# A two-layer graph network: second experts and first attention's end in another order, first mixture normalised by ScalarE and GpSimd

## The reference

```python
edge_index = jnp.stack([src, dst])                        # 8192 edges
xn = _layernorm(x)
x = x + _L0_gnn_ref(xn, edge_index, ...) + _L0_mix_ref(xn[None], ...)[0]
x = x + _L0_ffn_ref(_layernorm(x)[None], ...)[0]          # 16 experts, top 2
xn = _layernorm(x)
x = x + _L1_gnn_ref(xn, edge_index, ...) + _L1_mix_ref(xn[None], ...)[0]
x = x + _L1_ffn_ref(_layernorm(x)[None], ...)[0]          # 8 experts, top 2
# _L0_gnn_ref, 3 diffusion steps over the row-normalised adjacency
out = diffusion_weights[0] * h
for i in range(STEPS):
    cur = adj @ cur
    out = out + diffusion_weights[i + 1] * cur
return jax.nn.relu(out)
# _L0_mix_ref, the end: (out - mean) * rsqrt(var + EPS) * gamma
# _L1_gnn_ref: two graph attentions, each followed by
x_new = jax.nn.elu(_layer_norm(x_new, g, beta)); x = x + x_new
# _L1_ffn_ref, per token: gates * (gelu(x @ W1 + b1) @ W2 + b2) over its two experts
```

## Time and profile before

| | us |
|---|---|
| median of 3 timed runs | 223.85 |
| lowest and highest of them | 223.84, 232.37 |
| the profiled execution, its own time | 222.05 |
| span from its first to its last instruction | 220.3 |
| busy TensorE, VectorE, ScalarE, GpSimd in the span | 210.9, 141.2, 63.2, 22.1 |

### The profile page before, as it was taken

One profiled execution on the slowest core, in us unless ns is written; L12 is line 12 of the kernel. 1 busy time (PEld: TensorE's weight loads), 2 busy tenths in 40 slices (PEclk: granted clock), 3 DMA queues, 4 the chain that ended last, 5 costly groups with the idle time before them and its releaser, 6 DMA issues.

```text
span 220.3 us, 2936 instructions
## 1 busy us (share of the span) xinstructions
PE 210.9 (96%) x1031; PEld 142.9 (65%) x1031; DVE 141.2 (64%) x416; ACT 63.2 (29%) x148; POOL 22.1 (10%) x36
## 2 busy tenths in 40 slices
PE   7899999999999999999999999999959999999994
PEld 5685547666589988744646786478724564798641
DVE  3899999968998441432629259796934779653302
ACT  2804584322221012100101169730633321103100
POOL 4860010000111000000150000000300001200000
PEclk9999999999999999999999999999999999999969
DMA  5999799935050500000199000000000000000002
GB/s 164 355 394 358 238 404 416 412 118 176 1 190 4 190 0 3 0 0 0 44 297 405 18 0 1 3 0 0 0 0 3 0 0 0 1 3 0 0 0 95
DMA packets 8957, 23.65 MB, mean 107 GB/s; under 512 B 2408, under 2 KB 2408, under 8 KB 8944
## 3 DMA queue, kind: packets, MB, share of 16 engines
q1 hardware_dynamic: 8656, 23.42, 29.0%
q10 hardware_dynamic: 288, 0.07, 0.1%
HBM read 22.95 MB, written 0.52 MB: 107 GB/s over the span
## 4 chain that ended last, share of the span: by engine, by line
PE 84%; DVE 11%; issue 1%; DMA 1%; ACT 1%; POOL 0%; DVEq 0%
PE bank L1180 17%; PE bank L1154 12%; PE bank L1284 10%; PE bank L1272 10%; PE bank L1229 5%; PE bank L1315 4%; PE bank L1191 3%; PE bank L1235 3%; DVE ring L784 3%; PE bank L1329 2%; PE bank L1236 2%; PE bank L1168 2%; DVE ring L787 2%; PE bank L1220 2%; DMA xa<-in_x 1%
## 5 line engine op out<-in xcount | busy, mean ns | idle before, releaser
L1180 PE MATMUL bank<-raw,xT 128*128 128x512 f32 x88 | 39.3, 595 | 0.0
L1180 PEld LDWEIGHTS bank<-raw,xT 128*128 128x128 f32 x88 | 16.2, 190 | 18.3 <-issue 18.2
L301 POOL TENSOR_TENSOR rstd<-veps,minus_half 128x1 f32<-128x1 f32 x14 | 9.2, 660 | 153.2 <-DVE veps L561 111.1
L1315 PE MATMUL bank<-iota_bf 128*128 128x256 bf16 x155 | 21.5, 286 | 1.6 <-DVE iota_bf L760 1.6
L1284 PE MATMUL bank<-raw,ring 128*128 128x512 f32 x48 | 22.7, 633 | 0.0
L1272 PE MATMUL bank<-xT,raw 128*128 128x256 f32 x96 | 22.1, 384 | 0.0
L784 DVE TENSOR_SCALAR ring<-iota_bf,edges,radix 128x128 bf16<-128x128 bf16 x64 | 20.8, 376 | 0.0
L1315 PEld LDWEIGHTS bank<-iota_bf 128*128 128x128 bf16 x155 | 16.1, 107 | 5.2 <-DVE iota_bf L760 1.6
L1272 PEld LDWEIGHTS bank<-xT,raw 128*128 128x128 f32 x96 | 17.8, 190 | 2.3
L1284 PEld LDWEIGHTS bank<-raw,ring 128*128 128x128 f32 x48 | 9.6, 202 | 12.0 <-issue 11.6
L1191 PE MATMUL bank<-xT,raw 128*128 128x256 f32 x64 | 14.6, 382 | 0.2 <-issue 0.2
(11 more groups left out here) (256 smaller groups left out, 331.6 us busy)
## 6 DMA issues: line engine op xcount, KB each, us to landing
raw<-in_up SPq DMA_DIRECT2D x6, 512.0 KB, 10.6
raw<-in_down SPq DMA_DIRECT2D x6, 512.0 KB, 13.8
raw<-in_k SPq DMA_DIRECT2D x4, 512.0 KB, 5.5
raw<-in_q SPq DMA_DIRECT2D x4, 512.0 KB, 6.3
raw<-in_v SPq DMA_DIRECT2D x4, 512.0 KB, 6.9
raw<-in_out SPq DMA_DIRECT2D x4, 512.0 KB, 6.9
raw<-in_gat SPq DMA_DIRECT2D x4, 512.0 KB, 9.5
raw<-in_gnn SPq DMA_DIRECT2D x2, 512.0 KB, 10.0
```

The source lines that it names most:

```text
L1180: ins = mm(bank[banks[t]][:, :], xT_at(c, t), w.at(c), start=c == 0, stop=c == C - 1)
L1315: mm(half(b, 0), iota_bf[:, 0:P], iota_bf[:, :], start=True, stop=True)
```

## The change

In the first layer VectorE only takes the mixture's statistics and writes minus the mean. ScalarE centres the product and scales it by the root; GpSimd multiplies by `gamma0` and adds `xa`. ScalarE also makes the first term of `diffused`. TensorE's idle turns at the seam go from 29 to 11, and its attention-weight products change places with the first transposes. In the first attention's end VectorE's work is written tile by tile; `centred`, `normal`, `positive` and `negative` being one instruction each; the context product stands between the transposes of the two tiles, which go to other banks; ScalarE's exponentials move ahead. In the second experts the position products and the gates' transposes stand earlier among the `up1` products, 15 of 18 idle turns go, and half of `down1` precedes the bias rows. New semaphores and the tile `minus_mean`, and one-instruction helpers that only get a new argument, are left out below.

```diff
--- before.py
+++ after.py
@@ gpsimd
-            roots(1)
+            for t in range(T):
+                pool.wait_ge(var_ready, T + t + 1)
+                nc.gpsimd.tensor_tensor(rstd[:, t:t + 1], veps[:, t:t + 1], minus_half[:, t:t + 1], ALU.pow)\
+                    .then_inc(rstd_ready, 1)
+                pool.wait_ge(mix_scaled, t + 1)
+                then(nc.gpsimd.tensor_tensor(mixed[:, t, :], mixed[:, t, :], row["gamma0"], ALU.mult))
+                nc.gpsimd.tensor_tensor(mixed[:, t, :], mixed[:, t, :], xa[:, t, :], ALU.add).then_inc(mix_ready, 1)
             roots(2)
             roots(3)
@@ scalar, first layer
+            act.wait_ge(small_in, SMALLS)
+            for t in range(T):
+                nc.scalar.activation(diffused[:, t, :], hr[:, t, :], ACT.Copy, scale=diffusion[:, 0:1])\
+                    .then_inc(diffused_ready, 1)
             act.wait_ge(degree_ready, 1)
+            def mixture(t):
+                act.wait_ge(o_full, t + 1)
+                act.wait_ge(mean_ready, t + 1)
+                nc.scalar.activation(mixed[:, t, :], bank[t][:, :], ACT.Identity, bias=minus_mean[:, t:t + 1])\
+                    .then_inc(mix_centred, 1)
+                act.wait_ge(rstd_ready, T + t + 1)
+                act.wait_ge(mix_centred, t + 1)
+                nc.scalar.activation(mixed[:, t, :], mixed[:, t, :], ACT.Copy, scale=rstd[:, t:t + 1])\
+                    .then_inc(mix_scaled, 1)
+
             diffuse(0, (2, 7))
+            mixture(0)
             diffuse(1, (3, 4))
+            mixture(1)
@@ scalar, second layer
             mix_v(1, (5, 4), (0,))
+            elu(0, (0,))
             mix_v(1, (5, 4), (1,))
             for t in range(T):
                 act.wait_ge(ek_full, 2 + t + 1)
                 copy(ek[:, t, :], bank[2 + t][:, :]).then_inc(ek_ready, 1)
+            elu(0, (1,))
+            xT_part(3, 0)
             act.wait_ge(kinv_ready, 1)
             for m in range(C):
                 act.wait_ge(qT_full, 2 + m // 2 + 1)
                 nc.scalar.activation(qT[:, m, :], half(4 + m // 2, m % 2), ACT.Copy,
                                      scale=kinv[:, m:m + 1]).then_inc(qT_ready, 1)
-            elu(0, (0,))
 
             act.wait_ge(ctx_full, 2)
             for r in range(2):
                 p0, p1 = r * HD, (r + 1) * HD
                 copy(ctxbd[p0:p1, :, p0:p1], bank[3][p0:p1, :].rearrange("p (m n) -> p m n", m=C)[:, :, p0:p1])\
                     .then_inc(ctx_ready, 1)
-            elu(0, (1,))
-
-            xT_part(3, 4)
+
@@ vector, first layer
-            for t in range(T):
-                go(V.tensor_scalar(diffused[:, t, :], hr[:, t, :], diffusion[:, 0:1], None, ALU.mult))
...
                 variance(1, t, bank[t][:, :])
-                go(V.scalar_tensor_tensor(mixed[:, t, :], bank[t][:, :], mv[:, t, 0:1], row["gamma0"],
-                                          ALU.subtract, ALU.mult))
-                settle()
-                dve.wait_ge(rstd_ready, T + t + 1)
-                V.scalar_tensor_tensor(mixed[:, t, :], mixed[:, t, :], rstd[:, t:t + 1], xa[:, t, :],
-                                       ALU.mult, ALU.add).then_inc(mix_ready, 1)
+                V.tensor_scalar(minus_mean[:, t:t + 1], mv[:, t, 0:1], -1.0, None, ALU.mult).then_inc(mean_ready, 1)
 
             mixture(0)
+            dve.wait_ge(diffused_ready, T)
             diffuse(0)
             mixture(1)
             dve.wait_ge(step_read, 2)
             diffuse(1)
             dve.wait_ge(step_read, 4)
-            dve.wait_ge(mix_ready, 2)
 
             def residual(t):
                 dve.wait_ge(step_read, 4 + t + 1)
+                dve.wait_ge(mix_ready, t + 1)
@@ vector, second layer
+            def divided(u, t):
...
+                src = bank[AGG[t][u]][:, 0:4 * (HD + 1)].rearrange("p (h n) -> p h n", h=4)
+                dve.wait_ge(agg_full, 2 * u + t + 1)
+                go(V.reciprocal(mx[:, t, heads], src[:, :, HD]))
+                settle()
+                go(V.tensor_tensor(g_a[:, t, cols].rearrange("p (h n) -> p h n", h=4), src[:, :, 0:HD],
+                                   bc(mx[:, t, heads], [P, 4, HD]), ALU.mult))
+                settle()
+                go(V.tensor_tensor(g_a[:, t, cols], g_a[:, t, cols], row["b1"][:, cols], ALU.add))
...
             q_norm(1)
-            divided(0)
-            divided(1)
-            gat_norm(0, 4)
+            divided(0, 0)
+            divided(0, 1)
+            divided(1, 0)
+            settle()
+            variance(4, 0, g_a[:, 0, :])
+            divided(1, 1)
+            centred(0, 0)
+            normal(0, 0)
+            variance(4, 1, g_a[:, 1, :])
+            centred(0, 1)
             dve.wait_ge(xn_less_one, 1)
-            elu(0, x1g, lambda t: xn[:, t, :], xn, lambda ins: ins.then_inc(xn_ready, 1))
-            xT_part(3, 3)
+            positive(0, x1g, 0)
+            normal(0, 1)
+            negative(0, x1g, 0).then_inc(xn_ready, 1)
+            positive(0, x1g, 1)
+            negative(0, x1g, 1).then_inc(xn_ready, 1)
+            xT_part(3, 1)
@@ tensor, seam of the first layer
             attention_weights(0, 6, 0)
-            idle_turns(5, 7)
+            idle_turns(5, 3)
             attention_weights(0, 6, 1)
-            idle_turns(5, 7)
-            attention_weights(0, 6, 2)
             idle_turns(5, 3)
             pe.wait_ge(step_read, 4)
             xT_made(1, xn, (4, 5), (0,))
+            attention_weights(0, 6, 2)
+            idle_turns(5, 3)
             attention_weights(0, 6, 3).then_inc(wa_full, 1)
-            idle_turns(5, 12)
+            idle_turns(5, 2)
             xT_made(1, xn, (4, 5), (1,))
@@ tensor, end of the first attention
             qT_made((4, 5))
+            xT_made(3, x1g, (0, 1), (0,))
             pe.wait_ge(ek_ready, 4)
             context(3)
-            pe.wait_ge(qT_ready, 2 + C)
-            xT_made(3, x1g, (4, 3), (0,))
-            pe.wait_ge(ctx_ready, 4)
-            xT_made(3, x1g, (4, 3), (1,))
+            xT_made(3, x1g, (0, 1), (1,))
             node_rows(1, 7, 3)
             gat2 = Weight("gat2")
             weights_in(gat2)
+            pe.wait_ge(qT_ready, 2 + C)
+            pe.wait_ge(ctx_ready, 4)
@@ tensor, second experts
             logits(5, 1, 4)
-            up("up1", 0, 2)
-            up("up1", 2, 3, (0, 1))
+            up("up1", 0, 1)
+            up("up1", 1, 2, (0, 1))
             positions(1, 6)
-            up("up1", 2, 3, (2, 3))
+            up("up1", 1, 2, (2, 3))
+            up("up1", 2, 3, (0, 1, 2))
+            gate_rows(1, 7)
+            up("up1", 2, 3, (3,))
             up("up1", 3, C, (0, 1))
+            gate_spread(1, (2, 5))
             up("up1", 3, C, (2, 3))
-            idle_turns(2, 12)
-            gate_rows(1, 7)
-            idle_turns(2, 6)
-            gate_spread(1, (2, 5))
+            idle_turns(7, 3)
+            for t in range(T):
+                down("down1", t, bank[3 + t][:, :], C, 1, False, range(0, 2))
             pe.wait_ge(b_down_ready, 1)
             for t in range(T):
                 dst = bank[3 + t][:, :]
                 cols = slice(t * P, (t + 1) * P)
                 g_hi, g_lo = gateT_hi[0:EXPERTS[1], cols], gateT_lo[0:EXPERTS[1], cols]
-                mm(dst, g_hi, b_down_hi[:, :], start=True, stop=False)
+                mm(dst, g_hi, b_down_hi[:, :], start=False, stop=False)
                 mm(dst, g_hi, b_down_lo[:, :], start=False, stop=False)
                 mm(dst, g_lo, b_down_hi[:, :], start=False, stop=False)
-            for part in (range(0, 2), range(2, C)):
-                for t in range(T):
-                    down("down1", t, bank[3 + t][:, :], C, 1, True, part)
+            for t in range(T):
+                down("down1", t, bank[3 + t][:, :], C, 1, False, range(2, C))
```

More of the change, by code:

```diff
@@ L159, in gps_two_layers @@
         stats = sb("stats", [P, T, 6])
+        minus_mean = sb("minus_mean", [P, T])
         mv = sb("mv", [P, T, 2])
@@ L220, in gps_two_layers @@
             ["agg_full", "y_ready", "elu_exp", "out_ready", "stored"])
-        degree_ready = sem("degree_ready")
+        degree_ready, diffused_ready = sem("degree_ready"), sem("diffused_ready")
+        mean_ready, mix_centred, mix_scaled = sem("mean_ready"), sem("mix_centred"), sem("mix_scaled")
         kinv_ready, sign_loaded = sem("kinv_ready"), sem("sign_loaded")
@@ L1004, in _ @@
             edge_weights(3)
-            def gat_norm(g, i):
-                gg, beta = (("g1", "beta1"), ("g2", "beta2"))[g]
-                variances(i, lambda t: g_a[:, t, :])
-                for t in range(T):
[L1011 to L1026, removed]
-                    then(V.scalar_tensor_tensor(dst[:, t, :], g_b[:, t, :], 1.0, work[:, t, :], ALU.min, ALU.add))
+            def centred(g, t):
+                go(V.scalar_tensor_tensor(g_a[:, t, :], g_a[:, t, :], mv[:, t, 0:1], row[("g1", "g2")[g]],
+                                          ALU.subtract, ALU.mult))
```

(57 more changed lines are left out.)

3 lines of the change are left out of this document (2 added, 1 removed).

## The result

The changed kernel takes 225.55 us (median of 225.57, 225.55, 226.71, 225.52 and 225.43), the kernel before 223.85; the ratio is 1.0107, interval 1.0057 to 1.0157. So it is about 1% slower (0.8% by the two medians), less than 2%, and outside the predicted range of 217.3 to 221.7. Its profiled execution took 225.57 us for a span of 223.8.

A forecast was written before the change was run, and what follows sets the result against it. TensorE was taken to bound the kernel, with 84% of the time that sets the end. From the profiled execution, 222.05 - 1.7 - 1.89 - 0.4 + 0.2 + 1.3 = 219.6 us, range 217.3 to 221.7.

The forecast's parts named there:

- the fall at the seam: Seam between first graph part and experts: clock halves from about 70, costing 1.3 us (bounds 1.0 and 1.9); chance 0.48.
- the thin stretch from 159.70: First attention's end: PE busy 1.27 of 3.90 us at full clock, cited for the clock holding at the seam.
- a clock that holds: Rival at the seam: no fall there, 218.3 us, or 217.2 if GpSimd holds nobody either; chance 0.25.
- The fall at the end is spared: Second experts: the new order avoids the half-clock stretch behind the spread and bias rows, gain 1.89 us (bounds 0 and 1.89).
- Second experts: From the router's logits through `down1`: reordering and fewer turns gain 1.7 us, plus 1.89 for the spared clock fall.
- eighteen turns fewer: Sign for the second experts: eighteen idle turns fewer, with spread products about 3 us earlier.
- First attention's end: End of the first attention: tile-by-tile VectorE work and context between the transposes gain 0.4 us (bounds 0 and 1.2).
- GpSimd and the residual: Seam: GpSimd operations of 1.39 us hold VectorE's residual of tile 0 until 66.75, loss 0.2 us.
- the gain of 0.3: Seam: with GpSimd operations at 1.1 to 1.2 us, a gain of about 0.3 instead of the 0.2 loss.
- One fall more: Rival: the clock falls once more than in the trace, or the end's fall isn't spared, 221.4 or 221.5 us; chance 0.2.

The follow-up runs named there:

- the kernel with 18 more turns: The changed kernel with 18 more idle turns ahead of the first tile's transposes at the seam: 219.08, 220.84, 219.66 and 220.76 us, ratio 0.9837.
- the mixture alone: The kernel before with only the mixture moved to ScalarE and GpSimd: median 223.94 us over ten runs, ratio 0.998.
- the second experts alone: The kernel before with only the second experts' order changed: 222.59, 230.79, 219.11 and 222.63 us.
- the seam alone: The kernel before with only TensorE's new order and 11 turns at the seam, mixture still on VectorE: 229.55, 232.09, 231.79 and 223.94 us.
- the two parts: The kernel before with only the second experts and the first attention's end changed: 220.85, 220.5, 232.33 and 220.45 us, ratio 0.9854.
- the full products among the 16-row ones: Kernel before, second experts and first attention's end changed, two 128-row products put between 16-row broadcasts: 231.62, 221.19, 219.66, 221.27, 228.14 and 219.54 us.

## Why the prediction was wrong, point by point

**The step that failed is the price of the fall at the seam.** That it would come was forecast, as "slightly likelier than not", and by the clocks (0.969 or less) it came in all five runs. Its price was taken as 1.3, "bounds 1.0 and 1.9", from a fall behind which dense products stood ready. It was 4.69. A fall in a thin stretch stretches that stretch itself: products of 16 columns, turns and the router's logits took 1.6 to 1.8 times as long, and the half clock lasted until full products had run for 2.7 us. The one fall of the trace showed what a fall costs in dense work, not how long one lasts in thin work; its length was carried over to a place unlike it.

The Trainium skill, in TensorE: Matmul & The Clock Gate, section "Terms", prices a throttled time at its length times one less the share of pulses granted. The falls agree: 3.41 x 0.5 = 1.71 against 1.70 for the second one, and 10.24 x 0.5 = 5.12 against 4.69 at the seam. An estimate from the rows of the kernel with 18 more turns is that PE would have waited some 0.2 of that time anyway, ahead of 73.07; the rest of the difference is open. What a forecast lacks is the length.

**"For it, the thin stretch from 159.70"** was the case for a clock that holds. It rested on one execution. In the three other profiles with the old end of the first attention the clock falls at the end of that stretch or just behind it, for 3.41 us: from 165.85 in the mixture alone, 165.94 in the second experts alone and about 169.3 in the seam alone. In the nine profiles with the new end it does not. So the stretch was no sign that thin work is safe; and the new order of the first attention, priced at 0.4, seems to take away a fall as well, which neither the sum nor the table of three kernels holds.

**The fall at the end is spared**, as forecast: 209.00 to 213.00 stands at 1.00, and none of the ten profiles with the new order has a fall there. But the old order has it only in some executions: the seam alone has it (from 217.10), the mixture alone has not, with the same 8-row products in a row. So those products by themselves don't bring it, and that the profiled execution had this fall to lose was luck for the sum.

**Second experts: gain 2.87 instead of 1.7 + 1.89 = 3.59.** The chain of waits after, its end (start, us, what):

```profile
201.56 2.69 PE bank L1272 x12
...
208.88 0.42 DVE rows_lo L764
...
209.35 0.38 PE bank L1235
...
210.55 1.06 PE bank L1272 x4
...
215.38 0.43 PE bank L1583
215.80 0.23 PE bank L1584
...
216.97 3.64 PE bank L1284 x8
```

From 201.56 to 220.61 are 19.05, where the sum said 18.33; at full clock the old order took 20.04, so the work gains 0.99. Up to the spread products it is 7.79 against 7.63 (rows_lo comes last, as worked out). The other 0.6 lies behind: an instruction of 8 rows behind full products took longer than those that follow it (0.43 against 0.23 among the bias rows, whose first one took 0.23 behind the spread before), and the new order, which parts spread, `down1` and bias rows, pays that oftener: two products 1.06 for 0.88, bias rows 1.59 for 1.39, half of `down1` 3.64 for 3.44. (The "eighteen turns fewer" of the forecast are fifteen: three stand elsewhere, and its sum has them.)

**First attention's end: 0.4 forecast, 0.38 measured**, between the second transposes behind the first experts and those at its end. The context does stand between the two tiles' transposes (chain, after):

```profile
166.17 0.66 PE bank L1168 x4
166.83 1.79 PE bank L1154 x16
168.62 0.45 PE bank L1168 x4
```

**GpSimd and the residual: 0.2 forecast, 0.36 measured** where the clock holds. An operation takes 1.26 to 1.30 (taken 1.39), the residual is held, though otherwise than forecast: it starts at 65.61, takes 1.72 and ends at 67.33; second transposes 73.07 where 72.94 was forecast. The estimate of 1.1 to 1.2 an operation from the Trainium skill, GPSIMD Engine Reference, section "Elementwise — side-by-side cycle accounting", was about a tenth too low, and the gain of 0.3 by it did not come. What the Trainium skill says there, in section "Key points", of SBUF interfaces shared with VectorE, the hold of 1.72 against 0.69 bears out.

**One fall more** was a rival with 0.2. The profile has it, from 122.75, at 1.70. Such a fall needs nothing of the new seam: the profiles of the second experts alone, of the mixture alone and of the two parts have one at 118. But the changed kernel with PE's old order has a fall in two of eight runs at most; whether the seam's fall makes the second one likelier stays open. The kernel before, in its runs of 223.6 to 223.9, has a clock of 0.983 to 0.985, two falls, where its profiled execution had one. That is the 1.80 between that execution and the median, which the prediction left open. Where these two lie no profile shows; in the mixture alone, at the same clock, they lie at 118 and 166 and not at the end. Wherever they lie, if a fall costs about the same everywhere, median against median one fall is lost and one stays on either side: -2.87 - 0.38 + 0.36 + 4.69 = +1.80, measured +1.70. On the profiled execution's terms, with the second fall added, 222.05 + 1.80 + 1.70 = 225.55, measured 225.57.

So the second experts were 0.7 short, the other two parts within 0.2, the seam's fall 3.4 short, and the second fall (1.7) wasn't in the sum: 219.6 + 0.72 + 0.02 + 0.16 + 3.39 + 1.70 = 225.6. Without either fall, as in the run with 18 more turns, the changed kernel takes 219.1, below the forecast.

## What to carry to other kernels

Before idle turns or other filling work of TensorE are taken out, look at the stretch they stand in: where it is thin and long, a fall of the clock there stretches the thin work too: it cost 4.69 us at the seam, where the falls elsewhere cost 1.70 to 1.89. Put filling work where the engine waits anyway; here 18 turns in a wait cost nothing and kept 4.7 us. Don't take a stretch for safe because one execution ran it at the full clock. And compare a profile's clock with the clocks of the timed runs before a sum is made on one execution: a fall that one has and the others don't is a term by itself.

## What was unexpected, and what stays open

The clock fell, and stayed at half, while PE was busy: in the falls of 13.65 us and of 23.89 us PE is busy all the time (the rows of the seam alone and of the full products among the 16-row ones), and ahead of the fall of the kernel before it was busy 3.41 of 3.41. How many turns are enough isn't sharp. With the mixture on GpSimd, turns at the seam and the clocks of the timed runs: 11 turns, 0.962 to 0.969 in five runs; 20, 0.97, 0.97, 0.992, 0.977; 22, 0.977, 0.992, 1.0, 0.992; 29, in 22 runs of three kernels none under 0.982. Whether the turns count or only the wait that they fill, no run here parts: in the same order PE waits 2.34, 1.36, 1.15 and 0.33 to 0.37 us for the first tile. With VectorE's mixture and 25 to 29 turns, 5 of 18 runs of the experiments lie between 0.941 and 0.961. Whether that is due to the 0.33 us that PE waits there ahead of the third diffusion step, which GpSimd's mixture takes away, was not tried.

The residual, a VectorE instruction with two inputs in SBUF, waited for the GpSimd instruction that ran beside it (1.72 and 1.00 instead of 0.69), while the diffusion steps, with one input in PSUM, passed at 0.74 to 0.75 beside the same GpSimd work.
